# Sixteen-head cross attention: values transposed on four column groups, row sums and last key spread by one product per part, no fold

## The reference

```
qh = einsum('bshd,hed->bshe', q, wq) + bq      # h = 16 heads, d = 16
kh, vh = the same of the context (257 keys)
attn = softmax(einsum('bshd,bthd->bhst', qh, kh) / sqrt(16))
ctx = einsum('bhst,bthd->bshd', attn, vh)
out = ctx.reshape(b, s, 256) @ wo.T + bo
```

## Time and profile before

| | |
|---|---|
| median of three runs | 2012.2 us |
| span of the profiled execution | 2013.5 us |
| pipeline of the 32 tiles | up to about 1290 us |
| one slot, from the scores of half 0 to those of the next tile | 38.32 us |
| PE busy in that slot | 37.36 us |
| DVE, ACT, POOL busy in that slot | 28.70, 23.79, 14.95 us |

### The profile page before, as it was taken

How to read it: one execution, slowest core, us unless ns; L and a number is a source line. 1 busy time by engine, 2 the same in 40 slices (tenths; PEclk the granted TensorE clock), 3 DMA queues, 4 the chain that set the end, 5 groups by cost and what they waited for, 6 DMA issues and landing times. The chain is left out here.

```text
span 2013.5 us, 41473 instructions
## 1 busy us (share of the span) xinstructions
PE 1820.3 (90%) x11544; PEld 1354.2 (67%) x11577; DVE 1123.2 (56%) x3861; ACT 899.0 (45%) x2432; POOL 644.8 (32%) x1186
## 2 busy tenths in 40 slices
PE   3799999999989999999999999954999999999990
PEld 2577767777767767776776777742766776776670
DVE  4567767767767767676776777646121222222215
ACT  0466656656556656565665665512222222222220
POOL 0234334333433333343333434310322323223220
PEclk7899999999999999999999999975999999999995
DMA  9522222322222222222222310027111011010107
GB/s 326 194 84 84 86 74 82 95 74 73 91 79 81 80 81 82 77 87 74 94 75 75 94 59 12 7 116 296 60 34 34 31 34 34 31 34 31 34 27 255
DMA packets 115327, 169.72 MB, mean 84 GB/s; under 512 B 13440, under 2 KB 75392, under 8 KB 113088
## 3 DMA queue, kind: packets, MB, share of 16 engines
q1 hardware_dynamic: 108320, 148.80, 22.6%
q0 software_dynamic: 6816, 18.62, 2.9%
HBM read 137.10 MB, written 30.28 MB: 83 GB/s over the span
## 5 line engine op out<-in xcount | busy, mean ns | idle before, releaser
L725 ACT ACTIVATE x_prob<-ps,x_nmax 128x257 f32<-128x257 f32 x512 | 239.0, 472 | 238.3 <-DVE x_nmax L1026 237.8
L447 PE MATMUL ps<-context,x_probT 128*128 128x128 f32 x2048 | 275.9, 278 | 1.0 <-ACT x_probT L719 0.8
L447 PEld LDWEIGHTS ps<-context,x_probT 128*128 128x128 f32 x2048 | 259.7, 194 | 10.9 <-issue 2.5
L1378 PE MATMUL ps<-w,xeT 128*128 x568 | 257.2, 596 | 1.0 <-DVE xeT L1298 0.7
L1365 PE MATMUL ps<-w,heT 128*128 x1136 | 257.0, 379 | 1.0 <-DVE heT L1286 1.0
L1365 PEld LDWEIGHTS ps<-w,heT 128*128 128x128 f32 x1136 | 210.4, 190 | 27.3 <-issue 1.7
L1026 DVE TENSOR_REDUCE x_nmax<-ps 128x1 f32<-128x257 f32 x512 | 192.3, 416 | 41.8 <-PE ps L612 41.8
L719 ACT ACTIVATE x_probT<-ps 128x512 f32<-128x512 f32 x224 | 133.8, 598 | 150.4 <-PE ps L606 147.4
L790 POOL TENSOR_TENSOR x_lastv<-context,x_prob 128x128 f32<-128x128 f32 x256 | 121.0, 473 | 227.8 <-ACT x_prob L725 227.8
L606 PE MATMUL ps<-constants,x_prob 128*128 128x128 f32 x1024 | 164.2, 280 | 22.8 <-issue 21.4
L612 PE MATMUL ps<-context,query_blocks 64*128 64x257 f32 x1024 | 183.9, 437 | 0.0
(11 more groups left out here) (273 smaller groups left out, 3426.8 us busy)
## 6 DMA issues: line engine op xcount, KB each, us to landing
context<-in_cT SPq DMA_DIRECT2D x128, 257.0 KB, 2.9
context<-in_cn SPq DMA_DIRECT2D x128, 256.0 KB, 3.0
context<-in_lastk SPq DMA_DIRECT2D x128, 128.0 KB, 3.6
w<-in_m_w SPq DMA_DIRECT2D x16, 1024.0 KB, 20.5
yrows<-zero SPq DMA_DIRECT2D x1, 8192.0 KB, 29.0
w<-yrows SPq DMA_DIRECT2D x16, 512.0 KB, 6.1
xin<-in_x SPq DMA_DIRECT2D x32, 128.0 KB, 3.2
lastq<-in_lastq SPq DMA_DIRECT2D x32, 128.0 KB, 3.4
```

The lines of the kernel that those rows point to most:

```text
L447: t = mm(out, a, b, start=n == 0, stop=n == len(pairs) - 1)
L725: A(p1[kk % 2][:, g, :], ps[:, g, 0:KEYS], ACT.Exp, bias=nmax1[kk % 2][:, g:g + 1], accum_out=rsum1[kk % 2][:, g:g + 1]).then_inc(e1_ok.ha ...
L1378: t = mm(ps[:, 2 * b + n, :], xeT[b][:, k, :], w1[:, e, k, n * 512:(n + 1) * 512], start=k == 0, stop=k == H - 1)
```

## The change

- **Values transposed.** The weights are now 32 context channels (two heads), the moving operand 64 columns of `x_probT` (two heads times 32 tokens), and the output 32 partitions: eight products for a half, four (`j`) for each half of the keys, which go to the four groups of 32 columns of the array, j by j. The result is already transposed. Of the two heads in a 32x64 block two 16x32 corners are needed.
- **Parts.** Four halves make a *part* (`UNITS`), two parts a tile. The bank `B_V` collects the values of a part (256 columns), and beside them 256 columns with the last probability and the row sum of every (head, token), spread over the head's channels. For these ACT writes the row sum behind the probabilities, POOL multiplies the `fold` constant by both (`sums`, one operation of 128 elements for a half instead of two), and PE makes four products of 32 output partitions by 256 columns a part (`unit_sums`).
- **Post-processing.** `part_out` on DVE, once a part at the start of position 5 and (of the tile before) of position 1, takes six operations of 128x128: even heads by a parity mask, last key's share, reciprocal, odd heads, addition, product into `x_outT`. The per-half operations L1014, L1017, L1021, the fold and the copy L1031 are gone.
- **Loads.** `in_lastk` is no longer loaded; the last key is read from `in_cT`'s buffer. Sequences are loaded two at a time, when a part is through.

```diff
-            def unit_probs_T(t, m, k, K, folded):
-                if folded is not None:
-                    W(pe, f1_ok, folded[0] * NB, folded[2] // 2 + 1)
+            def unit_probs_T(t, m, k, K):
...
-            def unit_fold(t, m, k, K, last):
-                W(pe, om_ok, K, 1)
-                wait_probs_T(pe, last[0], last[2])
-                for h in (0, 1):
-                    i = mm(ps[:, B_T, h * S:(h + 1) * S], om[h][:].rearrange("p g d -> p (g d)"), const["fold"][:], start=True, stop=True)
+            def unit_values(t, m, k, K):
+                c, u = k // UNITS, k % UNITS
+                wait_probs_T(pe, t, k)
+                if u == 0:
+                    before = t * PARTS_OF_TILE + c - 1
+                    if not (isinstance(before, int) and before < 0):
+                        W(pe, post, before, POST.index("odd") + 1)
+                for n in range(KT):
+                    for j in range(GD // S * 2):
+                        g, pair = j // 2, j % 2
+                        i = mm(ps[j * S:(j + 1) * S, B_V, u * 2 * S:(u + 1) * 2 * S], cn[m][:, k // 2, n, k % 2 * P + j * S:k % 2 * P + (j + 1) * S],
+                               p1T[k % 2][:, g, n, pair * 2 * S:(pair + 1) * 2 * S], start=n == 0, stop=n == KT - 1)
+                i.then_inc(v1_ps.handle, 1)
+            def unit_sums(t, m, k, K):
+                W(pe, sums_ok, K, 1)
+                for j in range(GD // S * 2):
+                    g, pair = j // 2, j % 2
+                    i = mm(ps[j * S:(j + 1) * S, B_V, 2 * UNITS * S:], const["head_of_col"][:, pair * S:(pair + 1) * S],
+                           sums[k // UNITS][:, g].rearrange("p u s q -> p (u s q)"), start=True, stop=True)
...
-            def unit_values(t, m, k, K):
-                wait_probs_T(pe, t, k)
-                for g in (0, 1):
-                    i = product(ps[:, B_V, g * P:(g + 1) * P], [(p1T[k % 2][:, g, n, :], cn[m][:, k // 2, n, k % 2 * P:(k % 2 + 1) * P]) for n in range(KT)])
...
+            def part_out(t, m, k, K):
...
+                W(dve, f1_ps, n, 1)
+                done(v_.tensor_scalar(own[q][:], values[:, :, 0, :], const["parity"][:, 0:1], None, ALU.mult))
+                done(v_.tensor_tensor(lastv[q][:], spread[:, :, 0, :], lastkT, ALU.mult))
+                done(v_.reciprocal(rinv1[q][:], spread[:, :, 1, :]))
+                after("even")
+                done(v_.scalar_tensor_tensor(own[q][:], values[:, :, 1, :], const["parity"][:, 1:2], own[q][:], ALU.mult, ALU.add))
+                after("odd")
+                done(v_.tensor_tensor(own[q][:], own[q][:], lastv[q][:], ALU.add))
+                after("added")
+                done(v_.tensor_tensor(outT[m % 2][:, :, 2 * c * S:(2 * c + 2) * S].rearrange("p h (b q) -> p b h q", b=2),
+                                      own[q][:].rearrange("p (b h) q -> p b h q", b=2), rinv1[q][:].rearrange("p (b h) q -> p b h q", b=2), ALU.mult))
```

More of the change, by code:

```diff
@@ L379, in slot @@
                     load_x(*after)
[L380 to L384, removed]
-                        sp.dma_start(xnorm[known(done[0])], xn5[done[1] % 2][:]).then_inc(n_saved[done[1] % 2], 16)
-                    if b < NB - 1 and here and after:
-                        W(sp, om_ok, here[0] * HALVES, 2 * b + 2)
+                if done:
+                    W(sp, dve_s["self1"], done[0], "x5")
+                    sp.dma_start(xres[known(done[0])], x5[done[1] % 2][:]).then_inc(x_saved[done[1] % 2], 16)
+                if here and after:
+                    W(sp, post, here[0] * PARTS_OF_TILE, len(POST))
+                    for b in (0, 1):
                         load_batch(*after, b)
+                if done:
+                    W(sp, dve_s["router"], done[0], "norm")
+                    sp.dma_start(xnorm[known(done[0])], xn5[done[1] % 2][:]).then_inc(n_saved[done[1] % 2], 16)
             for t in range(RING):
@@ L633, in slot @@
                     if last:
-                        unit_probs_T(*last, oldest if oldest and oldest[2] % 2 == 1 else None)
+                        unit_probs_T(*last)
                     sl.steps(table, 2 * k)
@@ L718, in slot @@
                         W(act, t1_ps, K, 1)
+                        if not (isinstance(K, int) and K < 2):
+                            W(act, v1_ps, K - 2, 1)
                         A(p1T[kk % 2][:].rearrange("p g k t -> p (g k t)"), ps[:, B_T, :], ACT.Copy).then_inc(t1_rest.handle, 1)
@@ L789, in slot @@
                         W(pool, e1_ok, K, 2)
-                        tt(lastv[kk % 2][:], lastk[m][:, kk // 2, kk % 2 * P:(kk % 2 + 1) * P].rearrange("p (g d) -> p g d", g=2),
-                           p1[kk % 2][:, :, KEYS - 1:KEYS].broadcast_to([P, 2, GD]), ALU.mult).then_inc(lv_ok.handle, 1)
-                        W(pool, r1_ok, K, 1)
-                        tt(select[kk % 2][:], const["head_of_col"][:, kk % 2 * P:(kk % 2 + 1) * P].rearrange("p (g d) -> p g d", g=2),
-                           rinv1[kk % 2][:].unsqueeze(2).broadcast_to([P, 2, GD]), ALU.mult).then_inc(sel_ok.handle, 1)
+                        c, u = kk // UNITS, kk % UNITS
+                        earlier = t * PARTS_OF_TILE + c - 2
+                        if u == 0 and not (isinstance(earlier, int) and earlier < 0):
+                            W(pool, f1_ps, earlier, 1)
+                        tt(sums[c][:, :, u], const["fold"][:].unsqueeze(1).unsqueeze(1).broadcast_to([P, 2, 2, S]),
+                           p1[kk % 2][:, :, KEYS - 1:].unsqueeze(3).broadcast_to([P, 2, 2, S]), ALU.mult).then_inc(sums_ok.handle, 1)
                     sl.steps(table, 2 * k)
@@ L1040, in slot @@
                         v_.tensor_copy(p1T[0][:].rearrange("p g k t -> p (g k t)"), ps[:, B_T, :]).then_inc(t1_first.handle, 1)
-                    if last:
-                        unit_inverse(*last)
+                    if older and older[2] % UNITS == UNITS - 1:
+                        part_out(*older)
                     sl.steps(table, 2 * k)
```

85 lines of the change are left out of this document (38 added, 47 removed).

## The result

The changed kernel takes 2018.6 us, the median of five runs (2015.98 to 2020.85). The kernel before, run beside it, takes 2011.4 us (five runs, 2009.41 to 2012.77). The ratio is 1.0036 with a 95% interval from 1.0023 to 1.0048. So the change makes the kernel slower by 0.36%. The time lies inside the range of the prediction, but I gave "faster" a chance of 0.6, and that was wrong.

What follows compares the result with a forecast made beforehand. PE, busy 37.36 of 38.32 us, was taken to set the slot. Terms +0.65 - 1.00 + 0.02 + 1.03 - 0.44 - 0.90 = -0.64 us a slot, over 32 tiles -20.5, gave 1992 us; range 1940 to 2040.

Steps and rivals of the forecast that it cites:

- V: PE time for a half's values, two changes of shape included: 0.45 us forecast against 0.89 before, saving 0.44.
- The rival in which four groups don't keep up: On PE, small records paced by issue, values 0.65 us a half: 2043 us; chance 0.20 for 2012 to 2043.
- D: Length of the six-operation chain of `part_out` on DVE: 2.20 us forecast, bounds 1.50 and 2.45.
- Position 1 to 2: Stretch of the slot where `part_out` delays DVE's row maxima and so PE's transposes: loss of 0.65 us a slot.
- T(0): Start of PE's transposes of half 0, forecast unmoved; T(k) is that of half k.
- N(1): Start of DVE's row maxima of half 1, forecast 4.32 us after T(0) against 2.29 before; N(k) likewise for half k.
- Position 5: `part_out` delays `query_norm` on DVE by 1.47 us, PE gets back 0.44: loss of 1.03 us a slot.
- Position 3: PE saves 0.44 us on values and 0.56 on the removed fold, taken as gained in full: -1.00 us a slot.
- N(3) + 1.23: Earliest start of PE's transposes of half 3, 1.23 us behind DVE's row maxima; hanging on it would show the forecast wrong.
- Positions 6 and 7: PE's savings taken in full: values -0.44 us at 6, fold and values -0.90 us at 7.
- times 32 tiles: The slot's -0.64 us multiplied over all 32 tiles of the kernel: -20.5 us.
- the cheap burst: Rival: `part_out` on DVE takes only 1.50 us, 1.4 us a slot more gained, 1947 us; chance 0.17.

Runs made afterwards that it cites:

- run 2: Changed kernel with DVE inverting each half's two row sums before POOL spreads them, so `part_out` has no reciprocal; 2000.7 us, ratio 0.9947 to before.
- run 1: Changed kernel with the reciprocal of `part_out` replaced by a copy, so the division by row sums is left out; 2000.3 us, ratio 0.995 to before.
- run 6: Changed kernel with the early inversion of row sums and three unused PE products at position 1; 1979.9 us, ratio 0.9826 to before.
- run 7: Changed kernel with the early inversion of row sums and five unused PE products at position 1 instead of three; 1980.3 us, ratio 0.9837.
- run 4: Changed kernel with six unused PE products as filler at position 1; 2014.6 us, ratio 1.0003 to before.
- run 3: Changed kernel with four unused PE products as filler behind the scores at position 1; 2013.7 us, ratio 1.0008 to before.

## Why the prediction was wrong

**Right, and closely.** V: the block's 0.25 us (656.78 to 657.03) and two changes of 0.10 us were the forecast. After, a half followed by transposes takes 0.36 us, and the other change is now in the product ahead of it, which takes 0.52 us to the next start (661.58 to 662.10) for 0.43 before (623.54 to 623.97). V = 0.45 us, as forecast. The rival in which four groups don't keep up is dead: 16 records start within 0.25 us, 16 ns each, where the floor of 25 ns that the Trainium skill has (TensorE: Matmul & The Clock Gate, "Wait — 56ns, not 53.3ns?") would ask for 0.40 us. The trace doesn't agree with it for products on four column groups. The reciprocal took 0.95 us, against 0.98 from the line through the earlier trace rows; the 1.2 us estimated from the Trainium skill (VectorE: DVE Perf Modes, "First, the fixed hardware budget") was too high. D was 2.14 to 2.16 us for 2.20, the slot 37.77 for 37.7, the wait for `query_norm` 1.39 for "over 1". The wait at position 1 was not right: it is 2.62 us, and for `cross_norm`, where the forecast had 1.5 for `self_norm`.

**Terms that were off, and mostly cancelled.** The sum of the terms was -0.64 us, measured -0.47 against the mean of before's plain slots (38.24; the prediction took one slot of 38.32). That it came so near is luck in part, since two terms were too dark and one much too bright:
- Position 1 to 2: +0.65 forecast (its own 10.60 less 9.98 is 0.62), +0.32 measured (T(0)-T(2) 9.97 to 10.29). `cross_norm` and `self_norm` took 0.41 us each on DVE for 0.56 and 0.48 before, so N(1) came at T(0) + 4.10 (677.50 less 673.40) for the forecast 4.32. From N(1) to N(2) it was 4.97 us for 5.05, and T(2) = N(2) + 1.22 held.
- Position 5: +1.03 forecast, +0.63. `query_norm` started 1.30 us later behind T(4) than before and not 1.47, and took 0.39 us, not the 0.62 of the earlier trace rows.
- Position 3: -1.00 "gained in full" forecast, -0.25. This is the step of the slot's sum that failed: "PE works there without a wait now" was true before the change and not behind it. PE comes to the transposes of half 2 as early as the exponentials allow, and the next product then stands 0.35 us for `self_normT`, which ACT writes only behind the same exponentials and two copies of `cross_qT`. It ends at 646.96, and the product starts at 647.01, 1.09 us behind T(2); before it was 0.44 us (608.76 to 609.20 in that timeline). The timeline of ACT:

```profile
645.61 0.47 ACT L738 ACTIVATE x_prob<-ps,x_nmax 128x257 f32<-128x257 f32 x1
645.97 0.20 ACT L738 ACTIVATION_READ_ACCUMULATOR x_prob<-ps,x_nmax 128x1 f32 x1
646.06 0.62 ACT L693 ACTIVATE cross_qT<-ps,x_c 128x128 f32<-128x128 f32 x2
646.56 0.40 ACT L669 ACTIVATE self_normT<-ps 128x256 f32<-128x256 f32 x1
```

In slots of run 2 in which T(2) comes later because of the clock, this wait is absent (0.4 us in all for 6.3), and T(2)-T(3) is 6.43 us, 0.80 less than before: there the term is nearly what was forecast. The prediction named T(3) as a sign of being wrong, but by N(3) + 1.23; T(3) comes 3.18 us behind N(3) (649.72 to 652.90), so the sign pointed at the wrong engine. T(6) does lie at that limit, 1.25 us behind N(6) (665.80 to 667.05), at little cost.
- Positions 6 and 7: -0.44 and -0.90 forecast, -0.4 and -0.83.

**The step that decided the sign: "times 32 tiles".** A plain slot's -0.64 was taken for all 32 and from nothing else, so the last slots and the clock were put at nothing without a reason. Each is as large as the 4.8 us by which the plain slot was off (28 x 0.17), or larger:

1. *The end of the pipeline.* Where fewer layers run, nothing stands beside the block, and `s1_out` waits 2.29 to 2.38 us for `x_outT`, before 0.32 to 0.41. The last three slots lost 6.8 us. Shown by the rows of both tails, and by runs 1, 2, 6 and 7, where the shorter block gives the end back. The 1.9 us at the start are not the change's, as shown above. The forecast "none for `x_outT`" holds in plain slots only.
2. *The clock.* The windows of the earlier trace rows had 1.00, and I let it stay. Half-clock time grew by 49 us. The 28 middle slots should have given 28 x 0.47 = 13.2 us and gave 8.0. Of the missing 5.2 us 4.5 are in the plain slots that were longer than 37.77 us; one of them (600.88 to 639.55) begins with rows at half clock (0.69 us for 0.44), and with six products of filler (run 4) 3.8 of the 4.5 are back. By the medians, filler won back 4.9 us (run 3) and 4.0 (run 4). So some 4 to 5 us of the loss is the clock, and more where the waits are those of run 2 (20.8 us, run 6).

Together: -13.2 + 5.2 + 6.8 + 1.9 + 0.4 = +1.1 us, the two profiles' difference; the forecast of -20.5 us was 28 x -0.64 = -17.9, and 2.6 us more for the last four slots. The medians differ by 6 us more. Part of that is the draw of the profiled executions (before's was one of its longest, after's one of its shortest); what sets the clock of a single run is open. Without the start's 1.9 us the profiled pair would even be a small gain; that the change is slower rests on the medians, whose runs don't overlap (2012.77 at most before, 2015.98 at least after).

**Of the rivals**, the cheap burst is what run 1 imitates: 18 us came of the 45 forecast for it (1947 against 1992), since its slope assumed that both positions follow the block one to one while the clock stays; position 5 followed by half, and half-clock time grew by 26 us. The loads were rightly left at 0: `in_cT` and `in_cn` land in 3.8 and 4.2 us now instead of 2.9 and 3.0, but PE waits for neither.

**What stays open.** How much PE may stand before the clock falls isn't settled here: the rows show 2.6 us at position 1 in most plain slots of the changed kernel with the clock at 1.00, and 1.9 us in run 2, where it fell in nearly each slot. In the changed kernel the plain slots behind the ends of passes lose their clock for a while and the others don't, with the same wait. The spread of the slots at the ends of passes (42.0 to 44.7 us in run 4) has no cause here. Putting `part_out` behind the maxima at position 1 was not tried.

## What to carry to other kernels

Work taken from the engine that sets the pace counts only up to the next engine's order, so look at each place where the first engine would arrive early and ask what the second has in front of it, and do it for the last slots too, where no cover exists. A large operation on spread data (128 reciprocals a row) is worth moving ahead of the spreading (2 a row); here that was the difference between 2018.6 and 2000.7 us. Before a difference at the start of two profiles is put down to a change, look whether it lies ahead of the changed code. When PE gets idle, look at the granted clock behind each of its waits; 1.4 us of unused products in such a wait were worth 20.8 us here.

## What the runs showed of the hardware

- Waits in an otherwise busy slot lower PE's clock in some places and not in others. In run 2 the rows behind a wait of 1.90 us took 0.69 and 1.92 us for 0.44 and 1.03; with 1.4 us of filler in the wait they had the upper level again, 36.83 us a slot for 37.61.
- Eight products with weights of 128 rows by 32 columns and 64 moving columns (16 records) on four column groups start within 0.25 us. Twice as many take 0.47 us.
- A reciprocal on DVE with 2 elements a row took 0.16 us, with 128 elements 0.95 us; the other operations of 128 elements took 0.25 to 0.34 us.
- Three unused products (1.4 us) put ahead of two waits of 0.32 and 0.45 us in the kernel before lengthened that stretch by 0.14 to 0.19 us only.
- Two executions of the same code ahead of the first half can differ by 3 us at 65 to 69 us: 65.55 and 68.85 in the kernel before without and with filler, 65.30 and 68.70 in runs 3 and 4. The granted clock from 47 to 65.3 us was 0.78 and 0.85 in the early ones, 0.59 in the late ones.
